# The eight experts of a fused attention and expert kernel: gates multiplied into the activations, the second product as three split products summed in PSUM

## The reference

```python
logits = xf @ Wg
top_w, top_i = jax.lax.top_k(logits, TOP_K)          # TOP_K = 2 of E = 8 experts
top_w = jax.nn.softmax(top_w, axis=-1)
combine = einsum('nk,nke->ne', top_w, one_hot(top_i))
h = jnp.einsum('nc,ech->enh', xf, W1)                 # 128 -> 256, per expert
g = jnp.einsum('nc,ech->enh', xf, W2)
y = jnp.einsum('enh,ehc->enc', silu(h) * g, W3)       # 256 -> 128
out = jnp.einsum('enc,ne->nc', y, combine)
```

## Time and profile before

| what | value |
|---|---|
| median of 3 runs | 237.65 us (235.37 to 238.89) |
| the profiled execution | 236.75 us |
| its span, first to last instruction | 234.0 us |
| PE busy | 223.9 us, 96% |
| DVE, ACT, POOL busy | 167.4, 120.5, 69.9 us |
| chain that ended last | PE 81%, ACT 8%, DVE 8% |

### The profile page before, as it was taken

The page is one execution under the profiler, slowest core; times in us unless marked ns, Lnnn a source line. Parts: engine busy times, 40 slices in busy tenths (PEclk is TensorE's granted clock), DMA queues, the critical chain, the costliest instruction groups (busy, mean ns, idle before and its releaser), DMA issues.

```text
span 234.0 us, 5028 instructions
## 1 busy us (share of the span) xinstructions
PE 223.9 (96%) x1825; PEld 186.7 (80%) x1825; DVE 167.4 (72%) x433; ACT 120.5 (51%) x288; POOL 69.9 (30%) x105
## 2 busy tenths in 40 slices
PE   8999998899999999999999999999799999989994
PEld 8778888798886889888988989777578887766783
DVE  1688757898887895465555548988668889598763
ACT  2566949689753742233223224355445656757642
POOL 5625599042500308813125700360000000220200
PEclk9999999999999999999999999999979999999999
DMA  6870001000000010201202270000000000000002
GB/s 171 222 196 5 1 3 46 3 0 0 3 0 3 0 49 22 67 22 46 67 0 67 71 202 22 4 0 0 3 0 3 3 0 3 0 3 1 0 0 90
DMA packets 11868, 8.18 MB, mean 35 GB/s; under 512 B 3012, under 2 KB 11144, under 8 KB 11848
## 3 DMA queue, kind: packets, MB, share of 16 engines
q1 hardware_dynamic: 11848, 7.91, 12.4%
HBM read 5.81 MB, written 0.52 MB: 27 GB/s over the span
## 4 chain that ended last, share of the span: by engine, by line
PE 81%; ACT 8%; DVE 8%; issue 1%; POOL 0%; DVEq 0%; ACTq 0%; POOLq 0%
PE ps L676 11%; PE ps L478 9%; PE ps L850 9%; PE ps L480 8%; PE ps L479 8%; ACT probs L983 6%; PE ps L795 4%; PE ps L767 4%; PE ps L754 3%; PE ps L474 3%; PE ps L566 3%; PE ps L485 2%; PE ps L555 2%; PE ps L780 2%; PE ps L469 2%; DVE probs L1308 2%
## 5 line engine op out<-in xcount | busy, mean ns | idle before, releaser
L1040 ACT ACTIVATE kT<-ps 128x512 f32<-128x512 f32 x32 | 19.1, 598 | 47.1 <-PE ps L480 47.1
L676 PEld LDWEIGHTS ps<-w,kT 128*128 128x128 f32 x256 | 30.9, 192 | 1.3
L676 PE MATMUL ps<-w,kT 128*128 128x128 f32 x256 | 31.0, 275 | 0.0
L1384 DVE TENSOR_TENSOR kT<-ps,kT 128x512 f32<-128x512 f32 x32 | 21.8, 689 | 11.0 <-PE ps L480 8.7
L1391 DVE SCALAR_TENSOR_TENSOR x_sb<-ps,comb,x_sb 128x128 f32<-128x128 f32 x64 | 18.0, 344 | 13.5 <-PE ps L676 13.5
L478 PE MATMUL ps<-xT_hi,w_hi 128*128 128x512 f32 x64 | 26.5, 414 | 0.2 <-DVE kT L1384 0.2
L480 PE MATMUL ps<-xT_hi,w_lo 128*128 128x512 f32 x64 | 25.2, 394 | 0.0
L479 PE MATMUL ps<-xT_lo,w_hi 128*128 128x512 f32 x64 | 25.0, 391 | 0.0
L983 ACT ACTIVATE probs<-ps,negmax 128x128 f32<-128x128 f32 x64 | 22.6, 410 | 1.8 <-DVE negmax L1296 1.8
L1478 DVE TENSOR_REDUCE probs<-ps 128x8 f32<-128x1024 f32 x16 | 19.4, 1224 | 4.5 <-PE ps L754 4.3
L415 POOL TENSOR_TENSOR w_hi<-w_raw,zero 128x512 fp32r<-128x512 f32 x8 | 9.3, 1163 | 42.9 <-DMA w_raw<-in_L_ffn_W 28.2
(11 more groups left out here) (208 smaller groups left out, 512.3 us busy)
## 6 DMA issues: line engine op xcount, KB each, us to landing
w_raw<-in_L_ffn_W SPq DMA_DIRECT2D x16, 128.0 KB, 2.2
k_st<-h_a SPq DMA_DIRECT2D x12, 128.0 KB, 2.7
w<-in_L_ffn_W SPq DMA_DIRECT2D x8, 128.0 KB, 2.2
x_sb<-in_x SPq DMA_DIRECT2D x2, 256.0 KB, 5.4
ctx_sb<-in_ctx SPq DMA_DIRECT2D x2, 192.0 KB, 3.3
w_raw<-in_L_xattn_Wq SPq DMA_DIRECT2D x1, 256.0 KB, 5.3
wo<-in_L_xattn_Wo SPq DMA_DIRECT2D x1, 256.0 KB, 4.9
k_i<-in_L_ffn_k SPq DMA_DIRECT2D x1, 256.0 KB, 3.3
```

The costliest lines, as they stand in the source:

```text
L676: ins = pe.matmul(ps[:, 4 + slot, k * C:(k + 1) * C], uT[:, slot, c, k * P:(k + 1) * P], w3[:, buf, c, :], start=(c == 0), stop=(c == NH - 1))
L1040: act.activation(silu[:, c, :], ps[:, c, :], ACT.Silu).then_inc(b_silu, 1)
L1384: dve.tensor_tensor(uT[:, slot, c, :], ps[:, 2 + c, :], silu[:, c, :], ALU.mult).then_inc(b_u, 1)
```

## The change

- The gates go into the activations. `comb` is transposed (PE), copied (ACT), written to a small tensor in HBM (`comb_rows`), and read back for each unit from q = 4 on as a tile `comb_b` in which every partition has the 512 gates of that expert and half. `b_gate` becomes `u_chunk`: g times `comb_b`, then times `silu`, both on DVE, the second with both inputs in SBUF.
- The second product of units 4 to 15 is a split product with W3 stationary and u moving: per chunk high/high, low/high, high/low, six matmuls of 512 columns (`b_down`). It sums over the six experts of a half in one PSUM bank per half (`Y_ACC`), with the output's width on partitions. The high part of u is a copy on ACT (`u_high`); the low part of chunk 0 is made on DVE in units 4 to 11 and on POOL in units 12 to 15, that of chunk 1 on POOL in all. W3 is split as well, high on ACT (`down_high`), low on POOL (`down_low`). Units 0 to 3 (experts 0 and 1) stay as they were (`b_down_rows`).
- The order is by halves: six experts on half 0, then four of these backwards on half 1, then experts 3 and 2 again (`UNITS`), whose W1, W2 and W3 are loaded and split a second time: ten splits of W1 and W2 in place of eight. Split weights have four slots instead of two; slots 2 and 3 lie in `h_a`.
- At the end of a half the sum is copied (`y_copy`), transposed by four PE instructions (`b_turn`) and added (`y_add`). The layer norm of half 0 lies inside units 11 to 15: its scaling goes to ACT (`ln_scale(2, 0)`), its transposes stand between the two chunks of unit 15, and the ten `keep_busy` products are gone. All loops are unrolled.
- POOL: the third and fourth split no longer wait for a slot, so `k1_fill` follows them at once; the memsets of `qo` are cut up; the unpacking of `d1_w` and `d2_w` comes after the experts.
- In step s = 1 of the second attention `c_queries(6)` and its stacking move ahead of `c_scores(3, 0)` and its maximum.

```diff
@@ tables, new
+        JOBS = (0, 1, 2, 3, 4, 5, 6, 7, 3, 2)
+        SLOT = (0, 1, 2, 3, 0, 1, 2, 3, 3, 2)
+        UNITS = ((0, 0), (0, 1), (1, 0), (1, 1), (2, 0), (3, 0), (4, 0), (5, 0), (6, 0), (7, 0),
+                 (7, 1), (6, 1), (5, 1), (4, 1), (8, 1), (9, 1))
+        QN = 4
+        Q_LATE = 12
+        Y_ACC = (4, 5)
@@ SP
+            sp.wait_ge(b_combT, 1)
+            sp.dma_start(comb_rows[:, :], combT).then_inc(comb_out, 16)
+            sp.wait_ge(comb_out, 16)
+            for q in range(QN, QN + 4):
+                load_comb(q)
...
@@ POOL
+            def down_low(j):
+                pool.wait_ge(b_wh, j - 1)
+                hi, lo = down_split(j)
+                pool.tensor_tensor(lo, down_raw(j), f32(hi), ALU.subtract).then_inc(b_wl, 1)
+
+            def u_low(q, c):
+                n, s = q - QN, q % 2
+                pool.wait_ge(b_uh, NH * n + c + 1)
+                pool.tensor_tensor(u_lo[:, s, c, :], made[:, c, :], f32(u_hi[:, s, c, :]), ALU.subtract).then_inc(b_ul1 if c else b_ul0, 1)
...
-            pool.wait_ge(a_wo, NB)
-
-            for buf in range(2):
-                split_expert(2 + buf, buf)
+            pool.wait_ge(ln_lo, 2 * NT)
+            split_up(2)
+            split_up(3)
             pool.wait_ge(masks, 6)
             pool.tensor_copy(k_st[:, :, :].rearrange("p g n -> p (g n)"),
                              is_lo[:, 1:2].to_broadcast([P, NG * NB * P])).then_inc(k1_fill, 1)
@@ PE
+            def b_down(q):
+
+                (j, t), s, n = UNITS[q], q % 2, q - QN
+                first, last = q == min(i for i in range(QN, NU) if UNITS[i][1] == t), q == LAST[t]
+                if first:
+                    pe.wait_ge(b_acc, NT + QN)
+                pe.wait_ge(b_wl, j - 1)
+                hi, lo = down_split(j)
+                y = ps[:, Y_ACC[t], :]
+                for c in range(NH):
+                    pe.wait_ge(b_uh, NH * n + c + 1)
+                    pe.matmul(y, hi[:, c, :], u_hi[:, s, c, :], start=(first and c == 0), stop=False)
+                    pe.matmul(y, lo[:, c, :], u_hi[:, s, c, :], start=False, stop=False)
+                pe.wait_ge(b_ul0, n + 1)
+                pe.matmul(y, hi[:, 0, :], u_lo[:, s, 0, :], start=False, stop=False)
+                pe.wait_ge(b_ul1, n + 1)
+                pe.matmul(y, hi[:, 1, :], u_lo[:, s, 1, :], start=False, stop=last).then_inc(b_y, 1)
...
+            for q in range(QN, NU - 2):
+                b_down(q)
+                b_hidden(q + 2, (0,))
+                if q == LAST[0]:
+                    b_turn(0)
+                if q + 2 == NU - 1:
+                    ln_transposes(2, 0)
+                b_hidden(q + 2, (1,))
+            b_down(NU - 2)
+            b_down(NU - 1)
@@ PE, c_step
+                if s == 1:
+                    c_queries(NG + 2)
                 if s + 2 < NB:
                     c_scores(s + 2, 0)
                 if s == 1:
-                    c_queries(NG + 2)
                     c_queries(NG + 3)
@@ ACT
+            def u_high(q):
+                n, s = q - QN, q % 2
+                if n >= 2:
+                    act.wait_ge(b_y, q - 1)
+                for c in range(NH):
+                    act.wait_ge(b_u, NH * q + c + 1)
+                    act.activation(u_hi[:, s, c, :], made[:, c, :], ACT.Copy).then_inc(b_uh, 1)
...
+                if q == NU - 2:
+                    ln_scale(2, 0)
@@ DVE
+            def u_chunk(q, c):
+                n, v = q - QN, q * NH + c
+                dve.wait_ge(b_g, v + 1)
+                if c == 0:
+                    dve.wait_ge(ld_comb[q % 4], 16 * (n // 4 + 1))
+                if n == 0:
+                    dve.wait_ge(b_y, 3)
+                else:
+                    dve.wait_ge(b_uh, NH * (n - 1) + c + 1)
+                    dve.wait_ge(b_ul1 if c else b_ul0, n)
+                dve.tensor_tensor(made[:, c, :], ps[:, 2 + c, :], comb_b[:, q % 4, :], ALU.mult).then_inc(b_a, 1)
+                dve.wait_ge(b_a, NH * n + c + 1)
+                dve.wait_ge(b_silu, v + 1)
+                dve.tensor_tensor(made[:, c, :], made[:, c, :], silu[:, c, :], ALU.mult).then_inc(b_u, 1)
...
+            for q in range(QN + 1, NU):
+                u_chunk(q, 0)
+                if q == LAST[0] + 2:
+                    y_add(0)
+                if q == NU - 1:
+                    ln_low(2, 0)
+                u_chunk(q, 1)
+                if q < Q_LATE:
+                    u_low(q)
```

More of the change, by code:

```diff
@@ L162, in program @@
         relu = kT0[:, :, :].rearrange("p t (c n) -> p (t c) n", c=2)
+        made = kT0[:, 0, :].rearrange("p (c n) -> p c n", c=NH)
+        u_hi, u_lo = (h_c[:, i, :, :].rearrange("p (s c) n -> p s c n", c=NH) for i in range(2))
+        comb_b = probsT[:, :, :, :].rearrange("p s (i h) k -> p (s i) (h k)", i=2)
+        combT = o1[0:E * NB, :]
+        y_sb = ov[:, :]
         lgT = ctxT[0:E, :]
@@ L313, in _ @@
+            next_comb(10)
+            for j in (8, 9):
+                sp.wait_ge(b_wl, j - 5)
+                load_down(j)
+            for q in range(11, NU):
+                next_comb(q)
             sp.wait_ge(k1_fill, 1)
@@ L896, in _ @@
             pe.wait_ge(masks, 13)
-            for n in range(NG):
+            c_queries(0)
+            b_turn(1)
+            for n in range(1, NG):
                 c_queries(n)
@@ L1032, in _, with b_silu_step @@
             table(ACT.Silu)
-            def b_silu_step(q):
-                for c in range(NH):
+            def b_silu_step(q, chunks=range(NH)):
+                for c in chunks:
                     v = q * NH + c
@@ L1140, in d_evacuate @@
                     d_whole(n)
[L1142 to L1145 removed]
+            ln_scale(2, 1)
             ln_hi_copy(2, 1)
```

324 lines of the change are left out of this document (207 added, 117 removed).

## The result

The changed kernel takes 243.36 us (median of 4 runs, 242.31 to 243.96), the kernel before 236.74 in the same comparison (235.37 to 238.89); the ratio is 1.0297, 95% interval 1.0252 to 1.0341. The change makes the kernel 3% slower. The profiled execution took 242.31, its span 240.4 us, against 234.0 before. The ratios in this document leave out three executions that took over 1.5% more than the fastest of their kernel: one of e3 (247.79 us, mean clock 0.851) and two of the kernel before, timed beside e5 to e8 (238.53 and 238.72).

What follows compares the result with a forecast made beforehand. PE was taken to bound the kernel, busy 96% and fully so in the experts. The terms -2.1 + 2.6 + 4.3 - 2.1 + 1.6 = +4.3 on the profiled 236.75 gave 241.0 us, range 232.3 to 245.0.

Steps and rivals of the forecast that it cites:

- The start, +2.6: Before unit 2: POOL's later fill of `k_st` holds DVE's `gd`, and gates come later; 2.6 us more, bounds 0 and 3.
- Rival (b): At the start: the fill, reading one column, lets `gd` through and the rest holds; 236.8 us, chance 0.18.
- POOL and DVE in the units, +4.3: In the units: instructions with two SBUF inputs exclude each other; 3.0 in split units plus 1.3 in the last.
- Rival (a): POOL and DVE get out of each other's way and the fill does not hold DVE; 232.5 us, chance 0.22.
- PE's work, -4.9 and +0.5: In the experts: the new second product saves 0.41 in each of 12 units, 4.9; half 0's four transposes cost some 0.5.
- The end of the experts, -2.1: Units 11 to 15 to half 1's statistics: waits add 3.6, the closing chain takes 3.3 for 4.6; 148.8 against 150.94.
- The other two waits of this part, 1.3 and 1.5: Units 14 and 15: PE waits 1.3 for half 0's scaled x, and 1.5 in the last second product.
- The clock at the start, +1.6: Before unit 2: PE's new idle of over 2 us drops its clock, costing 1.6, bounds 0 and 3.2.
- Rival (c): At the start: all as forecast but PE's clock stays up; 239.4 us, chance 0.12.
- rival (d): In the units: exclusion costs 7, not 4.3, and waits in the last two drop the clock; 245.3 us, chance 0.12.
- Step s = 1, -2.1: Second attention: the query product moved ahead fills PE's 1.30 idle and the clock stays up; bounds -0.9 and -2.6.
- Rival (e): Step s = 1 brings only 0.9, because the clock falls for the idle left; 242.2 us, chance 0.06.

Runs made afterwards that it cites:

- e3: e2, with DVE's low part of chunk 0 in units 4 to 11 reading an idle PSUM bank, so wrong numbers: 237.46 us, ratio 1.0069.
- e5: The changed kernel with idle products on PE, eight ahead of unit 15's first chunk and four ahead of half 0's transposes: 243.84 us, ratio 1.0237.
- e8: e6 with half 0's norm refinement and `nm` after unit 14's products on DVE, its scaling and transposes also later: 235.35 us, ratio 0.9908.
- e1: The changed kernel with POOL's fill of `k_st` moved to right after the split of the second attention's query weights: 239.77 us, ratio 1.016.
- e2: The changed kernel with ACT writing silu back into its PSUM bank in units 4 to 15: 238.33 us, ratio 1.0109.
- e7: e6 without the seven DVE instructions that refine half 0's reciprocal root, so its scale stays the rough seed: 233.22 us, ratio 0.9817.
- e6: The changed kernel with the edits of e1 and e2 together: 235.95 us, ratio 0.9967.
- e4: The kernel before with only the change's reordering in step s = 1 (query product and its stacking moved ahead): 234.18 us, ratio 0.9918.

## Why the time came out near the forecast, and which steps were wrong

The forecast was 241.0, +4.3, with 0.59 on a time within 2% of the kernel before; the kernel came out 3% slower, for which it had 0.28, and the span grew by 6.4, 5.9 without the 0.5 from before the experts. The term for the experts' end was too low by over 3, and the clock was priced too high in another place, so part of the nearness is luck: two errors of opposite sign. One slip stands in the sum's frame: it adds to the profiled 236.75, but its 2% bounds, 232.9 and 242.4, are taken from the median of 237.65; from 236.75 they are 232.0 and 241.5.

**The start, +2.6: right up to unit 2, low behind it.** The 2.6 were 2.2 up to unit 2 (82.7 against 80.54) and 0.4 behind it for the gates. 2.2 were measured up to unit 2 (15.53 less 13.30), by the mechanism named: `gd` took 2.87 and ended with the fill, and e1 took the term away. Between units 2 and 5 it was 1.0, not 0.4 (98.00 less 83.28, 14.7, against 13.7 before). Rival (b), that a fill which reads one column lets `gd` through, is out.

**POOL and DVE in the units, +4.3: right in its sum, in part by luck.** e2 and e3 give 3.2 between the units and 1.1 in the tail, where the forecast had 3.0 and 1.3. But the 3.0 were to be four units with a split at 0.74 each, and units without a split were to fit. Against e3 the distance from start to start grew by 0.2, 0.7 and 0.1 in units 6 to 8 and by 0.3 and 0.7 in units 11 and 12, where splits run, 2.0 in all, and by another 0.8 and 0.4 in units 13 and 14, where no split runs but DVE has the norm to do as well. Only 0.4 of the whole is due to the low part on DVE. The mechanism, two SBUF inputs on DVE against a reading POOL, is shown by e2, which changed nothing but where silu lies. Rival (a), that the engines get out of each other's way, is out. The cut-up memsets of `qo` cost DVE's products nothing, as the sum had it. Timelines of POOL and DVE of the changed kernel, a memset beside a product with two SBUF inputs:

```profile
119.75 0.95 POOL L540 MEMSET qo<- 128x1024 f32 x1
...
119.84 0.69 DVE L1627 TENSOR_TENSOR kT<-kT 128x512 f32<-128x512 f32 x1
```

**PE's work, -4.9 and +0.5: right.** Where nothing waits, units of the changed kernel start 4.18 and 4.19 apart, in e2 and e3 also 4.13 and 4.14, against 4.54.

**The end of the experts, -2.1: wrong.** The step that failed is "The norm of half 0 on DVE (units 11 to 13) gives some 0.3", with the argument behind it that DVE by itself fits, 3.6 of 4.13. That sum held for a unit of five instructions and left out what the norm adds in units 11 to 13: the addition 0.68 and the statistics 0.87, the seed with its waits (134.85 to 137.39, 2.5), and the refinement with `nm`, 3.9 where POOL holds two of the nine; without the holds an estimate is 1.8, nine starts 0.20 apart. e7 prices the refinement at 1.7. Without it units 12 to 15 still start 4.53, 4.59 and 4.71 apart where 4.18 is the price of PE alone, 1.3 more. Of this 0.35 belongs to the exclusion and is counted there: in e3, with unit 11's low part free of POOL, the first of the three is 4.18. That the other 0.9 is the norm's is argued and not shown; it fits that the last of the three is 4.26 in e8, where `nm` stands behind unit 14's products. The forecast thus had 0.3 where some 2.6 stand. With the 1.0 between units 2 and 5 that makes 3.3 of the 3.4 by which this term was off.

The other two waits of this part, 1.3 and 1.5 in the last units, were sized well: in e7 it takes 9.06 from unit 15's start (138.76) to the matmul behind the last product (147.82), and 2.75 + 2 x 1.38 + 0.5 of work are in it, so 3.05 of waiting. The copy, the transposes, the addition and the statistics took 3.2 there; 3.3 had been forecast.

**The clock at the start, +1.6: wrong in place and size.** The clock stayed at 1.00 behind the idle of 2.44 in the profiled execution. In e5's, where it did fall, units 2 to 5 took 0.6 more. Rival (c) had this right. It fell in the tail instead, as the forecast's upper bound and rival (d) had it. There 7 us at a clock near half cost only 0.5 (13.84 from unit 15 to the statistics, against 13.33 in e1), since PE waits for ACT and POOL in the last unit; e5 kept the clock up and gained no more than that. In e6, which is lighter in these engines, the same fall cost 1.3 (13.52 against 12.22).

**Step s = 1, -2.1: right, against a profile at half clock.** -2.4 within the change and -2.0 in span alone (e4); the clock stayed up in both profiles. Half clock had cost 1.4 there, where the forecast had halved 3.3 to 1.65. Against the executions of the kernel before in which the clock stayed up anyway, e4 brings some 1.4 in span (231.6 against 233.0). Rival (e) is out.

The measured sum: 2.2 for the start, 0.5 that was there before the experts, 4.3 for the exclusion, 0.5 for the clock, and for the end of the experts with PE's work what remains of 8.8, +1.3 in place of -2.1. Less 2.4 for step s = 1 that is 6.4.

What stays open: why the clock falls behind one idle of 2.2 us and not behind another of the same length, and behind the idle of 1.30 in some executions of the kernel before and not in others. All four runs of the changed kernel had a mean clock of 0.977 to 0.986, those of e1 0.986 to 1.000 with the same idle.

## What to carry to other kernels

Before an elementwise operation is moved to DVE beside a working POOL, count its inputs in SBUF: here writing one operand in place in PSUM gave back 1.9% at no cost in instructions. Work that is "beside" the bound must be added up for each stage, with the small instructions and their waits: PE idled 2.2 us behind nine instructions on four columns, because they stood ahead of the products that it needed. Cut a change into its parts first: the one that paid here (0.8%) was a query product and its stacking moved ahead of a maximum, and it had nothing to do with the rest.
